# Four small moves around batch 0 of an adaLN block: row operations to GpSimd, exponentials ahead of q's seeds, far products ahead of a root, and ones in a TensorE wait

## The chip, the cores and the metric

The kernel runs as one program on one core of a Trainium2 chip. The metric is the device time of one execution in microseconds; the time before is the median of three runs. The four compute engines are TensorE (PE, with its weight loads as PEld), VectorE (DVE), ScalarE (ACT) and GpSimd (POOL). SyncE (SP) issues every DMA. Each engine takes its instructions in the order in which the program gives them, and waits only on semaphores.

## What is computed

Eight batches of 512 tokens with 256 features go through a modulated attention layer and a modulated, block-quantised linear layer:

```
mod = (silu(c) @ wmod).reshape(8, 6, 1, -1)
sa, ca, ga, sb, cb, gb = mod[:, 0] ... mod[:, 5]
ga = (2 * (ga >= 0) - 1) * maximum(abs(ga), 0.25)      # gb likewise
h = layernorm(x) * (1 + ca) + sa
x = x + ga * attention(h)      # 16 heads; only keys i and i - 2**k count, all others have score 0
h = layernorm(x) * (1 + cb) + sb
x = x + gb * (mx_quantize(h) @ mx_quantize(weight).T + bias)
```

Since each query sees only ten keys (offsets 0, 1, 2, 4 ... 256) beside a constant share of masked ones, the scores are ten elementwise products of q with a shifted k, summed over the 16 features of a head.

## The kernel before, in words

There is one loop over the batches, written out by hand for each engine, with the batches staggered: while the softmax of batch b is worked on, k, q and v of batch b + 1 and the transposes of batch b + 2 are made, and batch b - 1 is projected. What follows is the part around batch 0, where all edits lie.

**DVE.** It forms the products of batch 0 (`first_qk_products`, L1747), then `setup_rows` (L1711 to L1722): for all eight batches at once it takes the modulation rows out of PSUM and forms the clipped gates `rows8` and the gated biases `gated8`. These are operations on 8 partitions and 256 or 512 elements. Then comes `softmax_max(0)`: a maximum (L1833, tile `mx`) and, in two halves, the scores less that maximum (L1837). The maximum waits for the scores by token (`s_T`) and for both halves of `hT` of batch 1 (`s_hT` at 4). `softmax_weights(0)` (from L1850) waits for the exponentials, and `pv_product` (L1894) and `qk_product` (L1758) alternate after it.

**ACT.** After the scores and the two halves of `hT` of batch 1 (L1306), it seeds the banks of q with the bias (`seed_q(1)`, L1325), centres h of batch 1 (L1316, L1319), and only then enters the loop with `exps(0)` (em L1466, rest L1468, two halves L1471 and L1473). Then come `evacuate_k(1, ...)` (kT, L1332) and the statistics of batch 2: sums (L1231), squares (L1240), variance (L1244). The norm of batch 2 (x_norm, L1217) waits for POOL's root.

**POOL.** It splits the gated biases into three bf16 parts (`split_gated_biases`, L619 to L627), takes the root of batch 2 (`rstd_before(2)`: L662 with the operation pow, then L664), forms batch 0's two far products (`far_product`, L689: offsets 128 and 256), and adds up the products that DVE makes (`add`, L681). In batch b >= 1 the far products wait until TensorE has transposed the sums of batch b - 1 (`s_attp`).

**PE.** In batch 0 it makes k and q of batch 1 (L847, L858), v of batch 1 (L876), then waits for `x_norm` of batch 2 and transposes it (L834), turns one weight (L803), makes k of batch 2 (L847), and sums the products into scores of batch 1 (L980, L974, L994). `keep_busy` (L773) issues matmuls of ones whose result nobody reads.

**SP.** The DMA of the rows, `mod_rows<-x` (L510), stands behind the seven shifted loads of v.

The order on each engine is code order. The only things that couple them are the semaphores named here.

Of the kernel before, what the change touches and what calls it, by code (L numbers as in the profile page):

```python
# [5 lines left out]
ALU = mybir.AluOpType  # L6
# [20 lines left out]
def adaln_block(nc, x, wq, bq, wk, bk, wv, bv, wo, bo, wf, bf, cond, wmod, out):  # L27
    B, L, D = x.shape
# [41 lines left out]
    with ExitStack() as ctx:  # L70
# [24 lines left out]
        QUAD = 32  # L95
# [109 lines left out]
        s_wqk = sem("q_k_weights_transposed")  # L205
        s_xtile = sem("first_x_norm_tiles_by_scalar")
        s_xtiled = sem("first_x_norm_tiles_by_vector")
        s_split = sem("gated_biases_split")
        s_xin = sem("x_in_loaded")
        s_cols = sem("cols_loaded")  # L210
# [81 lines left out]
        CONST_EARLY = 7  # L292
        CONST_SUM = CONST_EARLY + 4 * NC
        CONST_ALL = CONST_SUM + NO + 1
        SETUP_SILU, SETUP_COLS, SETUP_WF, SETUP_MOD, SETUP_ROWS = 3, 5, 11, 12, 16
        PE_COND, PE_MOD, PE_WK, PE_COLS, PE_WQ, PE_WV, PE_ROWS, PE_WO, PE_WF = range(1, 10)
        NGATED = 5
        NLN1, NRS1, NLN2, NLN2D, NRS2 = 3, 2, 2, 3, 2
# [101 lines left out]
        def _(sp):  # L400
# [105 lines left out]
            for n in SHIFTED[1:]:  # L506
                shift_v(0, n)
            load_cols(2)
            sp.wait_ge(s_cset, SETUP_ROWS)
            sp.dma_start(rows_dram.ap(), rows8[:, :, :]).then_inc(s_spill, 16)  # L510
            sp.wait_ge(s_spill, 32)
            load_row_ga(0)
# [71 lines left out]
        def _(pool):  # L584
# [25 lines left out]
            for n in range(1, NO):  # L610
# [2 lines left out]
            nc.gpsimd.tensor_copy(fold[:, :].rearrange("p (y x h) -> p y x h", x=4, h=HC),  # L613
                                  ident[:, :].rearrange("p (x y h) -> p y x h", x=4, h=HC)).then_inc(s_const, 1)

            def split_gated_biases():

                pool.wait_ge(s_cset, SETUP_ROWS)
                nc.gpsimd.tensor_copy(split8[:, 0], gated8[:, :, :]).then_inc(s_split, 1)  # L619
                pool.wait_ge(s_split, 1)  # L620
                nc.gpsimd.tensor_tensor(rest8[:, :, :], gated8[:, :, :], split8[:, 0], ALU.subtract).then_inc(s_split, 1)
                pool.wait_ge(s_split, 2)
                nc.gpsimd.tensor_copy(split8[:, 1], rest8[:, :, :]).then_inc(s_split, 1)
                pool.wait_ge(s_split, 3)
                nc.gpsimd.tensor_tensor(rest8[:, :, :], rest8[:, :, :], split8[:, 1], ALU.subtract).then_inc(s_split, 1)
                pool.wait_ge(s_split, 4)
                nc.gpsimd.tensor_copy(split8[:, 2], rest8[:, :, :]).then_inc(s_split, 1)  # L627
# [82 lines left out]
            nc.gpsimd.memset(bias_att[:, :], 0.0).then_inc(s_bzero, 1)  # L710
            nc.gpsimd.memset(bias_ffn[:, :, :], 0.0).then_inc(s_bzero, 1)
            rstd_before(1)
            split_gated_biases()
            for b in range(LAST - 1):
                if has(b - 2):
                    rstd_after(b - 2)
                if has(b - 3):
                    dequantise_early(b - 3)
                if b == 0:
                    rstd_before(2)  # L720
                if b < EARLY:
                    far_product(b, 8)
                    far_product(b, 9)
                add(b, 1)
                if has(b - 2):
                    modulate(pool, nc.gpsimd, b - 2)
                if has(b - 3):
                    gate_ffn(b - 3)
                add(b, 2)
                add(b, 3)  # L730
                add(b, 4)
                add(b, 5)
                if has(b + 3):
                    rstd_before(b + 3)
                else:
                    rstd_after(b - 1)
                add(b, 6)
                if not has(b + 3):
                    dequantise_early(b - 2)
                add(b, 7)  # L740
                gate_projection(b)
# [23 lines left out]
        def _(pe):  # L765
# [371 lines left out]
            for b in range(LAST - 1):  # L1137
                ahead, post = has(b + 2), has(b - 3)
                q_rows(b + 1, 0)
                q_rows(b + 1, 1)  # L1140
                v_rows(b + 1, 1)
                if has(b - 1):
                    attention_transposes(b - 1)
                v_rows(b + 1, 0)
                if ahead:
                    h_transposes(b + 2, 1)
                    h_transposes(b + 2, 0)
                if b == 0:
                    weight_transposes(3)
                if has(b - 1):  # L1150
                    project(b - 1)
                if ahead:
                    k_rows(b + 2, 1)
                    k_rows(b + 2, 0)
                if post:
                    xd_transposes(b - 3)
                if b == 1:
                    weight_transposes(4)
                head_sums(b + 1, 0)
                if post:  # L1160
                    ffn(b - 3, 0)
                    ffn(b - 3, 1)
                head_sums(b + 1, 1)
                head_sums(b + 1, 2)
                scores_by_token(b + 1)
                if b in (0, 3):
                    v_means(means_of(b))
# [38 lines left out]
        def _(act):  # L1206
# [293 lines left out]
            copy_scores(0)  # L1500
            h_modulated(1, 1)
            h_modulated(1, 0)
            seed_q(1)
            centre_h(1)

            for b in range(LAST - 1):
                ahead, norm1 = has(b + 2), has(b + 3)
                exps(b)
                if b in (1, 4):
                    means_of_v(means_of(b - 1))  # L1510
                if b == 0:
                    evacuate_k(1, 1)
                    evacuate_k(1, 0)
                    sums_before(2)
                    squares_before(2)
                elif ahead:
                    norm_before(b + 2)
                if has(b - 2):
                    squares_after(b - 2)
                if has(b - 3):  # L1520
                    quantised(b - 3)
                evacuate_v(b + 1, 1)
                if b == 0:
                    norm_before(2)
                    evacuate_v(b + 1, 0)
                else:
                    evacuate_attention(b - 1)
                if has(b - 2):
                    norm_after(b - 2)
                if ahead:  # L1530
                    h_modulated(b + 2, 1)
                    h_modulated(b + 2, 0)
                if b == 0:
                    evacuate_weight(3)
                if norm1 and b > 0:
                    sums_before(b + 3)
                if has(b - 1):
                    take_x1(b - 1)
                if ahead:
                    evacuate_k(b + 2, 1)  # L1540
                    evacuate_k(b + 2, 0)
                if has(b - 3):
                    evacuate_xd(b - 3)
                    seed_ffn(b - 3)
                if ahead:
                    centre_h(b + 2)
                if b == 0:
                    sums_before(3)
                if norm1:
                    squares_before(b + 3)  # L1550
                if b == 1:
                    evacuate_weight(4)
                if not norm1:
                    squares_after(b - 1)
                if has(b - 3):
                    take_result(b - 3, 0)
                    take_result(b - 3, 1)

                copy_scores(b + 1)
                if ahead:  # L1560
                    seed_q(b + 2)
# [55 lines left out]
        def _(dve):  # L1617
# [87 lines left out]
            def setup_rows():  # L1705

                link, k = chain(s_cset, 0, 0)
                k[0] = SETUP_WF
                dve.wait_ge(s_pset, PE_ROWS)
                for i, m in enumerate((0, 3)):  # L1710
                    nc.vector.tensor_copy(gates[:, i, :], ps67[QUAD * m:QUAD * m + B, 0, 0:D])  # L1711
                nc.vector.tensor_copy(rows8[:, SB, :], ps67[QUAD:QUAD + B, 0, 0:D])
                link(nc.vector.tensor_scalar(rows8[:, CB, :], ps67[2 * QUAD:2 * QUAD + B, 0, 0:D], 1.0, None, ALU.add))
                assert k[0] == SETUP_MOD
                nc.vector.tensor_scalar(sgn[:, :, :], gates[:, :, :], 0.0, 2.0, ALU.is_ge, ALU.mult)
                link(nc.vector.tensor_scalar(mag[:, :, :], gates[:, :, :], -1.0, None, ALU.mult))
                link(nc.vector.scalar_tensor_tensor(out=mag[:, :, :], in0=gates[:, :, :], scalar=0.25,
                                                    in1=mag[:, :, :], op0=ALU.max, op1=ALU.max))
                link(nc.vector.scalar_tensor_tensor(out=rows8[:, GA:GB + 1, :], in0=sgn[:, :, :], scalar=-1.0,
                                                    in1=mag[:, :, :], op0=ALU.add, op1=ALU.mult))  # L1720
                dve.wait_ge(s_brow, 32)
                link(nc.vector.tensor_tensor(gated8[:, :, :], rows8[:, GA:GB + 1, :], brow[:, :, :], ALU.mult))  # L1722
                assert k[0] == SETUP_ROWS

            def setup_ffn_weight():
                link, k = chain(s_cset, 0, 0)
# [276 lines left out]
```

## Time and profile before

| | |
|---|---|
| median of three runs | 280.76 us (280.75 to 281.2) |
| the profiled execution's own time | 280.1 us |
| its span | 278.3 us |
| PE, DVE, ACT, POOL busy | 91%, 90%, 76%, 75% of the span |
| mean granted TensorE clock | 0.994 |

The profiled execution is 0.66 us shorter than the median, and 1.8 us of it lie outside the span. Busy shares are averages over the span; where a wait decides, the chain of work that ended last and the timelines of single engines say so.

### The profile page before, as it was taken

The page shows a single profiled execution, that of the slowest core. Times are in us where ns is not written, and L with a number is a line of the kernel's source. Part 1 is how long each engine was busy: PE and PEld are TensorE (multiplying, and loading weights), DVE is VectorE, ACT ScalarE, POOL GpSimd, SP SyncE. Part 2 cuts the span into 40 slices and gives each one's busy share as a digit, 9 for nine tenths or more (in the row PEclk, how much of TensorE's full clock was granted, in tenths as well). Part 3 has the DMA queues.
Part 4 walks back from the last instruction along what each step waited for, and adds up shares of the span by engine and source line. Part 5 has one row for each costly group of instructions (what it writes and reads, how often), then busy time and mean ns, then how long its engine had stood idle before and what let it go on. Part 6 is the DMA issues. An engine that isn't in the chain of part 4 may idle for free.

```text
span 278.3 us, 4396 instructions
## 1 busy us (share of the span) xinstructions
PE 253.6 (91%) x1356; PEld 162.7 (58%) x1356; DVE 249.4 (90%) x318; ACT 210.8 (76%) x564; POOL 209.4 (75%) x159
## 2 busy tenths in 40 slices
PE   6999996999999998799999999999999578997885
PEld 1754565258636843485568654766468445895664
DVE  3699899989998999999889998999984999999970
ACT  2377896785888896989889997998776736666753
POOL 6201339996998999999999899999999899945100
PEclk9999997999999999999999999999999999999999
DMA  7752996696695489327944796069803875730006
GB/s 226 191 194 78 297 312 179 205 351 196 212 320 182 141 273 319 127 98 252 341 143 132 221 361 197 19 204 364 247 1 116 255 212 180 227 133 15 0 5 224
DMA packets 54386, 53.90 MB, mean 194 GB/s; under 512 B 4094, under 2 KB 52812, under 8 KB 54364
## 3 DMA queue, kind: packets, MB, share of 16 engines
q1 hardware_dynamic: 54364, 53.63, 60.4%
q8 instruction: 11, 0.18, 0.3%
q14 instruction: 11, 0.09, 0.1%
HBM read 44.89 MB, written 8.72 MB: 193 GB/s over the span
## 4 chain that ended last, share of the span: by engine, by line
DVE 32%; PE 30%; ACT 14%; POOL 13%; issue 8%; DMA 1%; DVEq 0%; POOLq 0%; ACTq 0%
POOL pv_buf L681 7%; DVE prod L1758 6%; DVE pv_buf L1894 5%; PE ps L847 5%; PE ps L1111 5%; DVE prod L1894 4%; PE ps L1032 4%; DVE prod L1747 4%; PE ps L980 3%; ACT x_norm L1217 3%; ACT dump L1240 2%; PE ps L876 2%; POOL h L394 2%; POOL x_norm L389 2%; PE ps L834 2%
## 5 line engine op out<-in xcount | busy, mean ns | idle before, releaser
L681 POOL TENSOR_TENSOR pv_buf<-pv_buf 128x1024 f32<-128x1024 f32 x48 | 113.8, 2370 | 5.0 <-DVE pv_buf L1894 0.8
L1758 DVE TENSOR_TENSOR prod<-ps,kT 128x1024 f32<-128x1024 f32 (+4 forms) x70 | 75.0, 1107 | 0.0
L1894 DVE TENSOR_TENSOR pv_buf<-v_shift,ps 128x1024 f32<-128x1024 f32 x49 | 59.0, 1209 | 1.0 <-POOL pv_buf L681 1.0
L876 PE MATMUL ps<-wT,h_cen 128*128 128x256 f32 x128 | 29.9, 379 | 0.0
L847 PE MATMUL ps<-hT,wT 128*128 128x512 f32 x64 | 29.6, 603 | 0.0
L858 PE MATMUL ps<-hT,wT 128*128 128x512 f32 x64 | 29.4, 599 | 0.0
L876 PEld LDWEIGHTS ps<-wT,h_cen 128*128 128x128 f32 x128 | 23.9, 190 | 6.4 <-issue 3.8
L980 PE MATMUL ps<-prod,sel_sum 128*32 128x512 f32 x208 | 25.0, 598 | 2.0 <-DVE prod L1758 1.5
L1032 PE MATMUL ps<-wo_g,w_raw 128*128 128x256 f32 x112 | 26.4, 379 | 0.0
L662 POOL TENSOR_TENSOR rstd<-var,minus_half 128x4 f32<-128x4 f32 x8 | 8.1, 1017 | 20.5 <-ACT var L1244 19.0
L1032 PEld LDWEIGHTS ps<-wo_g,w_raw 128*128 128x128 f32 x112 | 21.2, 190 | 3.5
L858 PEld LDWEIGHTS ps<-hT,wT 128*128 128x128 f32 x64 | 11.7, 190 | 13.0 <-issue 12.4
L847 PEld LDWEIGHTS ps<-hT,wT 128*128 128x128 f32 x64 | 12.3, 198 | 11.9 <-issue 10.7
L1111 PE MATMUL ps<-wf_g,w_raw 128*128 128x256 f32 x80 | 18.7, 379 | 0.0
L670 POOL TENSOR_TENSOR rstd<-var,minus_half 128x4 f32<-128x4 f32 (+1 forms) x9 | 9.0, 998 | 11.5 <-ACT var L1285 8.8
L1332 ACT ACTIVATE kT<-ps,bias_cols 128x512 f32<-128x512 f32 x16 | 10.9, 687 | 8.7 <-PE ps L847 8.6
L1111 PEld LDWEIGHTS ps<-wf_g,w_raw 128*128 128x128 f32 x80 | 15.2, 190 | 2.3
L389 POOL TENSOR_TENSOR x_norm<-x_norm,rows_mod 128x1024 f32<-128x1024 f32 x6 | 14.2, 2365 | 1.9 <-ACT x_norm L1217 1.9
L1217 ACT ACTIVATE x_norm<-x_in,shift,rstd 128x256 f32<-128x256 f32 x28 | 14.5, 589 | 1.5 <-POOL shift L664 1.3
L1217 ACT ACTIVATE x_norm<-x,shift,rstd 128x256 f32<-128x256 f32 x28 | 14.5, 589 | 1.4 <-POOL shift L672 1.4
L394 POOL TENSOR_TENSOR h<-x_norm,rows_mod 128x1024 f32<-128x1024 f32 x6 | 14.2, 2362 | 0.5
L1306 ACT ACTIVATE hT<-ps,cols 128x512 f32<-128x512 f32 x16 | 12.2, 769 | 2.7 <-PE ps L821 2.0
(220 smaller groups left out, 570.7 us busy)
## 6 DMA issues: line engine op xcount, KB each, us to landing
v_shift<-v_rows SPq DMA_DIRECT2D x56, 512.0 KB, 5.5
x_in<-in_L_attn_x SPq DMA_DIRECT2D x8, 512.0 KB, 4.0
v_rows<-v_base SPq DMA_DIRECT2D x8, 512.0 KB, 3.0
x_res<-in_L_attn_x SPq DMA_DIRECT2D x8, 512.0 KB, 6.1
out_x<-outb SPq DMA_DIRECT2D x5, 512.0 KB, 4.7
rows_mod<-mod_rows SPq DMA_DIRECT2D x7, 256.0 KB, 6.1
x<-in_L_wmod SPq DMA_DIRECT2D x1, 1024.0 KB, 8.1
row_ga<-mod_rows SPq DMA_DIRECT2D x8, 128.0 KB, 3.0
```

Source lines behind the costliest of these rows:

```text
L389: ops.tensor_tensor(normed[:, t, :], normed[:, t, :], rows[:, 0:1, :].broadcast_to([P, n, D]), ALU.mult).then_inc(scaled, 1)
L394: ops.tensor_tensor(dst[:, t, :], normed[:, t, :], rows[:, 1:2, :].broadcast_to([P, n, D]), ALU.add).then_inc(done, 1)
L681: nc.gpsimd.tensor_tensor(dst, dst, ring(b, n)[:, t:NT, :], ALU.add).then_inc(s_add, 1)
L847: mm = nc.tensor.matmul(ps23[:, j, :], wT[:, 1, k, P * j:P * j + P], hT[:, k, :], start=(k == 1), stop=(k == 0))
L858: mm = nc.tensor.matmul(ps01[:, j, :], wT[:, 0, k, P * j:P * j + P], hT[:, k, :], start=False, stop=(k == NC - 1), skip_group_check=True)
L876: mm = nc.tensor.matmul(ps23[:, k2, col:col + D], h_cen[:, k, P * t:P * t + P], wT[:, 2, k, :], start=(t % 2 == 0 and k == 0), stop=(t % 2 ...
L980: mm = nc.tensor.matmul(ps23[32 * g:32 * g + 32, 1, :], sel_sum[:, which, c, :], prod[:, n, c, :], start=(c == 0 and which == 0), stop=(c ...
L1032: mm = nc.tensor.matmul(ps[:, k2, col:col + D], attnT[:, k, P * t:P * t + P], wo_by[b][:, k, :], start=False, stop=(t % 2 == 1 and k == NC ...
L1111: mm = nc.tensor.matmul(ps[:, half_, col:col + D], xdT_by[b][:, k, P * t:P * t + P], wf_by[b][:, k, :], start=False, stop=(t % 2 == 1 and ...
L1217: ins = nc.scalar.activation(dst[:, t, :], src[:, t, :], ACT.Identity, scale=rstd[:, t:t + 1], bias=shift[:, t:t + 1])
L1758: nc.vector.tensor_tensor(prod[:, n, :, o:L], ps01[:, :, o:L], kT[:, b % 2, :, 0:L - o], ALU.mult).then_inc(s_prod, 1)
L1894: nc.vector.tensor_tensor(dst[:, at, :].rearrange("p t (h e) -> p t h e", e=DH), v_n.rearrange("p t (h e) -> p t h e", e=DH), weights, ALU ...
```

## The change

Four edits, each in the setup or in the first two turns of the loop.

1. `setup_rows` on DVE ends two operations earlier. It now keeps twice the gate and a sign of plus or minus a half, so that the two remaining operations are plain products, and POOL does them: a new function `form_gates` with its own semaphore `s_gates`. SP's store of the rows waits for the first of them.
2. ACT does `seed_q(1)` and `centre_h(1)` after `exps(0)`, with the two halves of k between them.
3. POOL does `rstd_before(2)` after both far products and the first add of batch 0. In batch 1 the first add stands ahead of the far products.
4. PE issues six matmuls of ones after v of batch 1, ahead of the transposes of batch 2.

```diff
@@ sync
-            sp.wait_ge(s_cset, SETUP_ROWS)
+            sp.wait_ge(s_cset, SETUP_MOD)
+            sp.wait_ge(s_gates, 1)
@@ gpsimd
+            def form_gates():
+                pool.wait_ge(s_cset, SETUP_GATES)
+                nc.gpsimd.tensor_tensor(rows8[:, GA:GB + 1, :], sgn[:, :, :], mag[:, :, :], ALU.mult).then_inc(s_gates, 1)
+                pool.wait_ge(s_gates, 1)
+                pool.wait_ge(s_brow, 32)
+                nc.gpsimd.tensor_tensor(gated8[:, :, :], rows8[:, GA:GB + 1, :], brow[:, :, :],
+                                        ALU.mult).then_inc(s_gates, 1)
...
+            form_gates()
             split_gated_biases()
             for b in range(LAST - 1):
...
-                if b == 0:
-                    rstd_before(2)
+                if b == 1:
+                    add(b, 1)
                 if b < EARLY:
                     far_product(b, 8)
                     far_product(b, 9)
-                add(b, 1)
+                if b != 1:
+                    add(b, 1)
+                if b == 0:
+                    rstd_before(2)
@@ tensor
                 v_rows(b + 1, 0)
+                if b == 0:
+                    pe.wait_ge(s_d, 1)
+                    keep_busy(ps67, 0, 6)
@@ scalar
-            seed_q(1)
-            centre_h(1)
...
                 if b == 0:
+                    seed_q(1)
                     evacuate_k(1, 1)
+                    centre_h(1)
                     evacuate_k(1, 0)
@@ vector
-                    nc.vector.tensor_copy(gates[:, i, :], ps67[QUAD * m:QUAD * m + B, 0, 0:D])
+                    nc.vector.tensor_scalar(gates[:, i, :], ps67[QUAD * m:QUAD * m + B, 0, 0:D], 2.0, None, ALU.mult)
...
-                nc.vector.tensor_scalar(sgn[:, :, :], gates[:, :, :], 0.0, 2.0, ALU.is_ge, ALU.mult)
+                nc.vector.tensor_scalar(sgn[:, :, :], gates[:, :, :], 0.0, 0.5, ALU.is_ge, ALU.subtract)
...
-                link(nc.vector.scalar_tensor_tensor(out=rows8[:, GA:GB + 1, :], in0=sgn[:, :, :], scalar=-1.0,
-                                                    in1=mag[:, :, :], op0=ALU.add, op1=ALU.mult))
-                dve.wait_ge(s_brow, 32)
-                link(nc.vector.tensor_tensor(gated8[:, :, :], rows8[:, GA:GB + 1, :], brow[:, :, :], ALU.mult))
```

On ACT, between the second half of `hT` and the first sum of batch 2, stood before (`ps<-bias_cols` are q's seeds, `em` to the second `ps<-score_buf` are the exponentials):

```order
18 L1306 ACTIVATE hT,h_sum<-ps,cols 128x512 x2
19 L1325 ACTIVATE ps<-bias_cols 128x512 x2
20 L1316 ACTIVATE h_off<-h_sum 128x2
21 L1319 ACTIVATE h_cen<-hT,h_off 128x512 x2
22 L1466 ACTIVATE em<-mx 128x64
23 L1468 ACTIVATE ps<-em 128x4x16
24 L1471 ACTIVATE ps<-score_buf 128x2x160
25 L1473 ACTIVATE ps<-score_buf 128x2x160
26 L1332 ACTIVATE kT<-ps,bias_cols 128x512 x2
27 L1231 ACTIVATE dump,sum<-x_in 128x256 x4
```

In the same place of the changed kernel stands:

```order
18 L1323 ACTIVATE hT,h_sum<-ps,cols 128x512 x2
19 L1483 ACTIVATE em<-mx 128x64
20 L1485 ACTIVATE ps<-em 128x4x16
21 L1488 ACTIVATE ps<-score_buf 128x2x160
22 L1490 ACTIVATE ps<-score_buf 128x2x160
23 L1342 ACTIVATE ps<-bias_cols 128x512 x2
24 L1349 ACTIVATE kT<-ps,bias_cols 128x512
25 L1333 ACTIVATE h_off<-h_sum 128x2
26 L1336 ACTIVATE h_cen<-hT,h_off 128x512 x2
27 L1349 ACTIVATE kT<-ps,bias_cols 128x512
```

The number of instructions ahead of the sums is the same; the exponentials, which wait for DVE's maximum, are now the first of them.

On POOL, from the splits of the gated biases to the second root of the loop, stood before (`rstd` and `shift` are a root):

```order
39 L619 CAST split<-h 8x512
40 L621 TENSOR_TENSOR h<-h,split 8x512
41 L623 CAST split<-h 8x512
42 L625 TENSOR_TENSOR h<-h,split 8x512
43 L627 CAST split<-h 8x512
44 L662 TENSOR_TENSOR rstd<-var,minus_half 128x4
45 L664 TENSOR_TENSOR shift<-negmean,rstd 128x4
46 L689 TENSOR_TENSOR far_buf<-v_base,score_buf 128x768
47 L689 TENSOR_TENSOR far_buf<-v_base,score_buf 128x512
48 L681 TENSOR_TENSOR pv_buf<-pv_buf 128x1024 x5
```

and now stands:

```order
39 L620 TENSOR_TENSOR x<-outb 8x512
40 L623 TENSOR_TENSOR h<-x,zq 8x512
41 L629 CAST split<-h 8x512
42 L631 TENSOR_TENSOR h<-h,split 8x512
43 L633 CAST split<-h 8x512
44 L635 TENSOR_TENSOR h<-h,split 8x512
45 L637 CAST split<-h 8x512
46 L699 TENSOR_TENSOR far_buf<-v_base,score_buf 128x768
47 L699 TENSOR_TENSOR far_buf<-v_base,score_buf 128x512
48 L691 TENSOR_TENSOR pv_buf<-pv_buf 128x1024
49 L672 TENSOR_TENSOR rstd<-var,minus_half 128x4
50 L674 TENSOR_TENSOR shift<-negmean,rstd 128x4
```

Two products are new ahead of the splits, and the root went from ahead of the far products to behind them and one add.

## Rows read from the trace of the kernel before

**Rows 1.** Page, granted TensorE clock in 40 slices of the span.
```profile
PEclk9999997999999999999999999999999999999999
```

**Rows 2.** Chain of work that ended last, 30 to 60 us: start, us, what.
```profile
30.88 0.95 ACT hT L1306 x3
...
40.88 1.01 POOL rstd L662
...
50.73 0.04 ACT kT L1332
...
56.96 0.59 ACT score_buf L1482
```

**Rows 3.** Timeline of ACT, 31 to 62 us: start, us, operation, [idle before <-releaser].
```profile
31.73 1.11 ACT L1325 ACTIVATE ps<-bias_cols 128x512 f32<-128x512 f32 x2
...
34.23 0.24 ACT L1466 ACTIVATE em<-mx 128x64 f32<-128x64 f32 x1
...
35.38 1.24 ACT L1332 ACTIVATE kT<-ps,bias_cols 128x512 f32<-128x512 f32 x2
36.52 0.41 ACT L1231 ACTIVATE dump<-x_in 128x256 bf16<-128x256 f32 x1
...
40.59 0.20 ACT L1244 ACTIVATE var<-sq 128x4 f32<-128x4 f32 x1
...
45.47 0.78 ACT L1306 ACTIVATE hT<-ps,cols 128x512 f32<-128x512 f32 x1 [0.73 <-PE ps L834]
...
60.99 0.40 ACT L1348 ACTIVATE v_mean<-ps,bias_cols 128x3 f32<-128x3 f32 x2
```

**Rows 4.** Timeline of DVE, 30 to 61 us.
```profile
30.69 0.68 DVE L1719 SCALAR_TENSOR_TENSOR x<-outb 8x512 f32<-8x512 f32 x1
...
32.12 0.89 DVE L1833 TENSOR_REDUCE mx<-ps 128x64 f32<-128x704 f32 x1
...
35.22 0.50 DVE L1850 TENSOR_TENSOR ps<-ps,em 128x320 f32<-128x320 f32 x1 [1.29 <-ACT ps L1471]
...
58.77 0.89 DVE L1833 TENSOR_REDUCE mx<-ps 128x64 f32<-128x704 f32 x1 [0.78 <-PE ps L1011]
...
60.79 0.50 DVE L1850 TENSOR_TENSOR ps<-ps,em 128x320 f32<-128x320 f32 x1 [0.21 <-ACT ps L1471]
```

**Rows 5.** Timeline of POOL, 32 to 64 us.
```profile
32.15 0.60 POOL L619 CAST split<-h 8x512 bf16<-8x512 f32 x1 [7.41 <-DVE h L1722]
...
35.93 0.60 POOL L627 CAST split<-h 8x512 bf16<-8x512 f32 x1
...
42.11 2.51 POOL L689 TENSOR_TENSOR far_buf<-v_base,score_buf 128x768 f32<-128x768 f32 x2
44.59 12.43 POOL L681 TENSOR_TENSOR pv_buf<-pv_buf 128x1024 f32<-128x1024 f32 x5
...
63.19 1.27 POOL L639 TENSOR_TENSOR wo_g<-wT,row_ga 128x512 f32<-128x512 f32 x1
```

**Rows 6.** Timeline of SP's queue, the store of the rows.
```profile
36.09 0.35 SPq L510 DMA_DIRECT2D mod_rows<-x  x1
```

**Rows 7.** Timeline of PE: transposes, the wait before batch 2, ones and a wait near the end.
```profile
29.51 1.09 PE L834 MATMUL ps<-ident,x_norm 128*128 128x128 f32 x8
...
44.32 1.97 PE L834 MATMUL ps<-ident,x_norm 128*128 128x128 f32 x8 [2.53 <-ACT x_norm L1217]
...
219.67 0.38 PE L1081 MATMUL ps<-bias_ffn,ones 128*128 128x512 bf16 x1 [2.00 <-ACT ps L1428]
...
258.36 0.82 PE L773 MATMUL ps<-ones 3*128 3x512 bf16 x3
```

**Rows 8.** Windows: stretch, us, busy time of PE, PEld, DVE, ACT, POOL, granted clock, DMA share, GB/s.
```profile
43.75:44.00 0.25, 0.00 (x0) 0.00 (x0) 0.25 (x1) 0.25 (x2) 0.25 (x1) 0.67 0.61 201
44.00:47.00 3.00, 2.68 (x13) 2.68 (x14) 3.00 (x4) 2.27 (x5) 2.94 (x2) 0.50 0.73 197
...
47.25:50.75 3.50, 3.50 (x12) 1.29 (x15) 3.50 (x4) 1.23 (x3) 3.36 (x2) 1.00 1.03 354
```

More of the change, by code:

```diff
@@ L207, in adaln_block @@
         s_xtiled = sem("first_x_norm_tiles_by_vector")
+        s_gates = sem("gates_formed")
         s_split = sem("gated_biases_split")
@@ L294, in adaln_block @@
         CONST_ALL = CONST_SUM + NO + 1
-        SETUP_SILU, SETUP_COLS, SETUP_WF, SETUP_MOD, SETUP_ROWS = 3, 5, 11, 12, 16
+        SETUP_SILU, SETUP_COLS, SETUP_WF, SETUP_MOD, SETUP_GATES = 3, 5, 11, 12, 14
         PE_COND, PE_MOD, PE_WK, PE_COLS, PE_WQ, PE_WV, PE_ROWS, PE_WO, PE_WF = range(1, 10)
@@ L614, in _ @@
                                   ident[:, :].rearrange("p (x y h) -> p y x h", x=4, h=HC)).then_inc(s_const, 1)
+            def form_gates():
[5 more added lines that the diff above has]
+                                        ALU.mult).then_inc(s_gates, 1)
             def split_gated_biases():
-                pool.wait_ge(s_cset, SETUP_ROWS)
+                pool.wait_ge(s_gates, 2)
                 nc.gpsimd.tensor_copy(split8[:, 0], gated8[:, :, :]).then_inc(s_split, 1)
@@ L1714, in setup_rows @@
                 assert k[0] == SETUP_MOD
-                nc.vector.tensor_scalar(sgn[:, :, :], gates[:, :, :], 0.0, 2.0, ALU.is_ge, ALU.mult)
+                nc.vector.tensor_scalar(sgn[:, :, :], gates[:, :, :], 0.0, 0.5, ALU.is_ge, ALU.subtract)
                 link(nc.vector.tensor_scalar(mag[:, :, :], gates[:, :, :], -1.0, None, ALU.mult))
-                link(nc.vector.scalar_tensor_tensor(out=mag[:, :, :], in0=gates[:, :, :], scalar=0.25,
+                link(nc.vector.scalar_tensor_tensor(out=mag[:, :, :], in0=gates[:, :, :], scalar=0.5,
                                                     in1=mag[:, :, :], op0=ALU.max, op1=ALU.max))
-                link(nc.vector.scalar_tensor_tensor(out=rows8[:, GA:GB + 1, :], in0=sgn[:, :, :], scalar=-1.0,
-                                                    in1=mag[:, :, :], op0=ALU.add, op1=ALU.mult))
-                dve.wait_ge(s_brow, 32)
-                link(nc.vector.tensor_tensor(gated8[:, :, :], rows8[:, GA:GB + 1, :], brow[:, :, :], ALU.mult))
-                assert k[0] == SETUP_ROWS
+                assert k[0] == SETUP_GATES
             def setup_ffn_weight():
```

## The prediction

> **What bounds the kernel now.** I read the chain of work that ended last first, from the end of batch 0's scores to the scores of batch 1, since all edits lie there. It runs through ACT, not DVE: from the second half of hT, which ends at 31.83, ACT works without a gap through q's seeds, centring, exponentials, k and batch 2's statistics up to the variance at 40.59 [rows 2, 3]. POOL's root follows at 40.88, ACT's norm, and PE's transposes of batch 2 at 44.32 [rows 2, 7]. From there the chain goes through k of batch 2 (kT at 50.73) and the next statistics on ACT to the copy of batch 1's scores at 56.96 [rows 2]. DVE is not on it: ahead of the maximum of batch 1, at 58.77, it has been idle for 0.78 us, waiting for PE's transposes of those scores [rows 4]. A microsecond saved on DVE before that point only makes this wait longer. A microsecond lost on ACT ahead of the root goes straight into the end.
>
> Then the clock. It dips once in the whole span, in the seventh slice [rows 1]. PE had been idle for 2.53 us before 44.32 [rows 7]. In the stretch 43.75 to 44.00 the mean is 0.67, so it fell to its lower level, 1.2 GHz, at about 43.8, two microseconds into the wait; it stays at 0.50 to about 47.25 and is back at 1.00, 2.4 GHz, after it [rows 8].
>
> **The change, part by part.**
>
> *Two operations off DVE.* They took 32.12 - 30.69 = 1.43 us [rows 4]. But the maximum also needs hT, done at 31.83 [rows 2]; add some 0.05 for the signal, and it starts at 31.9 in place of 32.12. The cut is worth 0.2 us of its 1.43.
>
> *Exponentials first on ACT.* ACT is free at 31.83, where q's seeds start at 31.73 today by overlap [rows 3]. Now em has to wait for the maximum: 31.9 + 0.89, so 32.8. ACT stands still for 1.1 us where it had no gap. In batch 1, where the exponentials also meet DVE at work, the ACT operation behind them starts 60.99 - 58.77 = 2.22 us after the maximum [rows 3, 4]; here that is 34.1. Before, the exponentials took ACT 35.38 - 34.23 = 1.15 us, seeds and centring 34.23 - 31.73 = 2.50, k 36.52 - 35.38 = 1.14 [rows 3]. The sums of batch 2 therefore start at 34.1 + 2.50 + 1.14 = 37.75 against 36.52, and the variance is there at 42.0 against 40.79: a loss of 1.25 us on the chain. For DVE the move is a gain: L1850 came 2.02 us after the maximum in batch 1 [rows 4], so at 33.9 here against 35.22, 1.3 us earlier. Seeds now end near 34.7 and 35.2; the matmuls of q that add to them are behind k on PE and start at about 34.7, so nothing waits there by more than 0.1 us (PE is reckoned as busy up to 44.32 - 2.53 = 41.79 either way [rows 7]).
>
> *Row operations on POOL.* The gates are ready for POOL at 30.7 [rows 4]. A product of 512 elements took POOL 1.27 us [rows 5], on 128 partitions; the split, on 8 partitions, ran five operations from 32.15 to 36.53 [rows 5], 0.6 to 1.2 each. I take 1.2 to 1.3 for each product, 2.5 for both. The split then runs 33.2 to 37.6. SP's store of the rows went out at 36.09, behind the loads of v [rows 6], and its input is now there at 32; the store of the split biases is behind it in the same queue. Nothing on SP moves.
>
> *Root behind far products and an add.* POOL does the far products at 37.7 (42.11 to 44.59, so 2.48 us [rows 5]), and the add (12.43 / 5 = 2.49 us [rows 5]). That is the root at 42.65. The variance would have let it start at 42.1; the order costs 0.5 more. In all the root moves from 40.88 to 42.65, by **1.77 us**, and so do norm and transposes: PE starts on batch 2 at 46.1. The other five adds of batch 0 get ahead of their old places by 3 us, but the root of batch 3 stands in front of the last two and waits for ACT, as it nearly does today. The exchange in batch 1 starts an add while the far products would wait for PE; POOL then meets the root of batch 4, which waits for ACT again. Both are worth nothing.
>
> *Ones.* Three took 0.82 us at the full clock, so 0.22 each after the first [rows 7]; six end at 43.1, inside the wait. They cost nothing on the chain. They leave PE idle from 43.1 to 46.1, 3.0 us.
>
> *What the clock is worth.* From the transposes to kT of batch 2 takes 50.73 - 44.32 = 6.41 us [rows 2, 7]. PE worked for 2.7 to 2.9 us of it at 0.50 [rows 8]; at 1.00 this is 1.35 to 1.45 less. The eight transposes show it: 1.97 against 1.09 [rows 7]. Part of it is hidden, since k's matmuls also wait for hT from ACT (0.78 for a half [rows 3]), which does not get faster. I take 1.25.
>
> A rule of the Trainium skill bears on this ("TensorE: Matmul & The Clock Gate", Part 4: PE-mode transpose): transposes don't count as TensorE activity as matmuls do, so they would not bring the clock back. The trace does not agree: most of the work between 44.32 and the return at 47.25 was transposes. By the rule a low stretch would last longer here; the fourth case below is that one.
>
> **The sum.** With the clock held: +1.77 - 1.25 = +0.5 us. With a second fall in the longer wait, as now: +1.77 if the low stretch lies as it does today, and +0.5 + 1.7 = +2.2 if it comes fully under work (3.4 us at half speed costs 1.7; today 0.5 of it is spent idle). Behind 57 us everything follows ACT and PE as today, so this goes to the end unchanged.
>
> **The cases.**
>
> 1. *The clock falls again*, chance 0.53, +1.8 to +2.2. For it: an idle stretch of 2.53 us lost the clock after two [rows 7, 8], and this one is 3.0 us, after ones that use 3 of 128 rows of the array. Against it: a wait of 2.00 us near the end did not lose it [rows 7, 1], and where in a wait it falls is known from one fall only. The profiled execution, 280.1, would become 282.1; the median stands 0.66 above it, which gives **282.7**. Its own range is 282.0 to 283.4.
> 2. *The ones hold the clock*, chance 0.30: +0.5, so 281.3, from 280.7 to 281.8, just about the 0.2% (0.56 us) that a measurement of this kernel can tell from no change.
> 3. *Faster*, chance 0.10. The mechanism is DVE's 1.3 us reaching the end, with the clock held. It needs the copy of batch 1's scores before 56.4, hence transposes of batch 2 at full clock before 45.0 and the root before 41.6: the sums would have to start by 37.3, and POOL to be free 1.1 us earlier than reckoned. This happens if the maximum does not have to wait and the 8-partition products take next to nothing. At most 1.3 us: 279.5.
> 4. *A long low stretch*, chance 0.07: the clock falls in the wait and stays low through all of k of batch 2. The 3.5 us of matmul after 47.25 [rows 8] would take up to 7, on top of case 1: up to +5, 285.5.
>
> **Range and chances.** Slower by over 0.2%: all of cases 1 and 4 and a little under half of case 2, 0.73. Within: the rest of case 2 and a part of 3, 0.17. Faster: 0.10. The range goes from 280.6, below case 2's value, to 283.8, above that of case 1; it leaves out most of cases 3 and 4.
>
> **What the changed profile would show.** The maximum of batch 0 near 31.9, with ACT idle for 1 us before em; L1850 near 33.9. The first sum of batch 2 near 37.75, the root near 42.65 with POOL busy up to it, transposes of batch 2 near 46.1, PE idle for 3 us before them. DVE's wait ahead of batch 1's maximum grows from 0.78 to over 2.5. The windows of 43 to 51 us decide between cases 1, 2 and 4: a low granted clock or none. The forecast is wrong if ACT does not stand still ahead of em, if the root comes before 42, or if no low clock appears after the ones.

## The result and the profile after

The changed kernel takes 286.16 us (285.32 to 286.47, four executions) against 280.75 for the kernel before: a ratio of 1.0191, 95% interval 1.0165 to 1.0217. The prediction was 282.7, with a range to 283.8: the right side, but the loss is 5.4 us and not 2. Executions of one kernel here differ mostly by how often the TensorE clock fell in them, so the mean granted clock stands beside times below where it matters; in all four executions of the changed kernel it was 0.976.

Page of the changed kernel, span and granted clock in 40 slices:

```profile
span 284.5 us, 4409 instructions
PEclk9999997978999999999999999999999999999799
```

[rows 1] had one dip; here are three places: the seventh slice, the ninth and tenth, and one near the end.

DVE of the changed kernel, its timeline:

```profile
32.12 0.89 DVE L1846 TENSOR_REDUCE mx<-ps 128x64 f32<-128x704 f32 x1 [1.31 <-ACT hT L1323]
...
34.14 0.50 DVE L1863 TENSOR_TENSOR ps<-ps,em 128x320 f32<-128x320 f32 x1 [0.21 <-ACT ps L1488]
...
61.63 0.89 DVE L1846 TENSOR_REDUCE mx<-ps 128x64 f32<-128x704 f32 x1 [4.71 <-PE ps L1025]
...
89.56 0.89 DVE L1846 TENSOR_REDUCE mx<-ps 128x64 f32<-128x704 f32 x1 [3.14 <-PE ps L1025]
```

The maximum of batch 0 starts at the same 32.12 [rows 4]: it waited 1.31 us for hT, so most of the 1.4 us cut from DVE turned into a wait. (hT itself ended 0.16 us later in this execution, 31.99 against 31.83, ahead of any of the edits; the run with the row operations alone, below, has the maximum 0.14 us earlier.) L1863 (L1850 before) is 1.1 us earlier. All of that, and 2.9 us more, is spent in the wait ahead of batch 1's maximum, 4.71 us against 0.78.

ACT and POOL, their timelines:

```profile
33.04 0.26 ACT L1483 ACTIVATE em<-mx 128x64 f32<-128x64 f32 x1 [1.06 <-DVE mx L1846]
...
42.05 0.20 ACT L1261 ACTIVATE var<-sq 128x4 f32<-128x4 f32 x1
...
59.08 0.58 ACT L1499 ACTIVATE score_buf<-ps 128x512 f32<-128x512 f32 x1
```

```profile
30.89 1.27 POOL L620 TENSOR_TENSOR x<-outb 8x512 f32<-8x512 f32 x1 [6.31 <-DVE outb L1734]
32.24 1.26 POOL L623 TENSOR_TENSOR h<-x,zq 8x512 f32<-8x512 f32 x1
...
40.40 2.37 POOL L691 TENSOR_TENSOR pv_buf<-pv_buf 128x1024 f32<-128x1024 f32 x1
42.73 1.01 POOL L672 TENSOR_TENSOR rstd<-var,minus_half 128x4 f32<-128x4 f32 x1
```

ACT stands still for 1.06 us ahead of em, the variance comes at 42.05 to 42.25, and the root at 42.73, right behind the add (40.88 in [rows 2]). The copy of batch 1's scores, L1499, is at 59.08 against 56.96 [rows 2].

PE's timeline of the changed kernel, two rows of the kernel before in the same place, and windows of the changed kernel with the columns of [rows 8]:

```profile
42.12 1.46 PE L787 MATMUL ps<-ones 3*128 3x512 bf16 x6
46.18 1.97 PE L848 MATMUL ps<-ident,x_norm 128*128 128x128 f32 x8 [2.60 <-ACT x_norm L1234]
...
54.48 1.92 PE L988 MATMUL ps<-prod,sel_sum 128*32 128x512 f32 x16
56.19 1.06 PE L1008 MATMUL ps<-prod,sel_sum 128*32 128x512 f32 x8
59.71 1.02 PE L1020 MATMUL ps<-ident,score_buf 128*128 128x128 f32 x4 [2.45 <-ACT score_buf L1499]
...
62.95 5.52 PE L872 MATMUL ps<-hT,wT 128*128 128x512 f32 x8
```

```profile
52.36 3.87 PE L974 MATMUL ps<-prod,sel_sum 128*32 128x512 f32 x16
...
57.59 0.66 PE L1006 MATMUL ps<-ident,score_buf 128*128 128x128 f32 x4 [0.50 <-ACT score_buf L1482]
```

```profile
46.50:49.50 3.00, 3.00 (x13) 2.64 (x12) 3.00 (x4) 2.27 (x6) 2.86 (x2) 0.50 0.96 302
50.00:57.25 7.25, 7.25 (x47) 2.25 (x45) 6.91 (x7) 5.00 (x15) 3.73 (x2) 1.00 0.57 195
57.25:59.50 2.25, 0.01 (x2) 0.00 (x0) 0.00 (x0) 2.22 (x10) 0.25 (x1) 1.00 1.12 344
60.00:66.50 6.50, 6.50 (x20) 4.44 (x19) 4.53 (x9) 4.77 (x13) 6.28 (x5) 0.50 0.86 273
265.00:268.00 3.00, 3.00 (x8) 2.31 (x7) 2.86 (x7) 2.48 (x7) 1.34 (x2) 0.50 0.00 0
```

The first low stretch, 46.2 to 49.6, lies wholly under work; in the kernel before it began inside the wait.

The new event is the second wait. PE begins batch 1's sums 2.1 us late (52.73 against 50.62), but they take it 4.5 us and not 6.5: in the kernel before it had to wait for DVE's products among them (3.87 us for L974, 1.92 for the same L988 now). So they end at 57.25, nearly as before (57.09), while ACT copies the scores 2.1 us later, at 59.08. PE idles for 2.45 us where it idled for 0.5, and then works from 60.0 to 66.5 at 1.2 GHz. Eight matmul instructions of q take 5.52 us where they took 3.7 in the kernel before.

How the 6.2 us of span come about, by landmarks of the two profiles: kT of batch 2 at 52.84 against 50.73 (+2.1), maximum of batch 1 +2.9, maximum of batch 2 at 89.56 against 84.15 (+5.4), unchanged up to batch 6, and the rest at the end, where a third low stretch lies under matmuls.

### The profile page after: what moved, and what is told of

The parts are those of the page before. It is cut to its first block, busy times and chain, and to the rows that moved or that the text cites. A ratio compares the mean times of both kernels' runs of the same rounds, so it can differ in the third digit from the quotient of the medians.

```text
span 284.5 us, 4409 instructions
## 1 busy us (share of the span) xinstructions
PE 257.3 (90%) x1362; PEld 166.0 (58%) x1362; DVE 248.0 (87%) x316; ACT 211.3 (74%) x564; POOL 211.9 (74%) x161
## 4 chain that ended last, share of the span: by engine, by line
PE 34%; POOL 22%; ACT 15%; DVE 15%; issue 11%; DMA 2%; SPq 0%; POOLq 0%; ACTq 0%; DVEq 0%
POOL pv_buf L691 11%; PE ps L1125 6%; PE ps L861 6%; DVE prod L1907 4%; PE ps L1046 4%; ACT x_norm L1234 3%; PE ps L994 3%; DVE prod L1771 3%; PE ps L872 2%; POOL x_norm L390 2%; DVE pv_buf L1907 2%; ACT dump L1298 2%; ACT dump L1257 2%; DMA pv_buf<-in_L_wmod 2%; PE ps L890 2%
## 5 line engine op out<-in xcount | busy, mean ns | idle before, releaser
L872 PE MATMUL ps<-hT,wT 128*128 128x512 f32 x64 | 31.3, 632 | 0.0
L861 PE MATMUL ps<-hT,wT 128*128 128x512 f32 x64 | 29.4, 600 | 0.1
L1125 PE MATMUL ps<-wf_g,w_raw 128*128 128x256 f32 x80 | 20.0, 397 | 0.0
L861 PEld LDWEIGHTS ps<-hT,wT 128*128 128x128 f32 x64 | 12.1, 195 | 11.9 <-issue 10.7
L1125 PEld LDWEIGHTS ps<-wf_g,w_raw 128*128 128x128 f32 x80 | 16.2, 203 | 2.9 <-issue 0.3
L1846 DVE TENSOR_REDUCE mx<-ps 128x64 f32<-128x704 f32 x8 | 7.1, 891 | 11.1 <-PE ps L1025 9.6
L1358 ACT ACTIVATE v_base<-ps 128x512 f32<-128x512 f32 x16 | 9.3, 588 | 7.8 <-PE ps L890 6.7
```

Of the source, the lines that this page charges most:

```text
L861: mm = nc.tensor.matmul(ps23[:, j, :], wT[:, 1, k, P * j:P * j + P], hT[:, k, :], start=(k == 1), stop=(k == 0))
L872: mm = nc.tensor.matmul(ps01[:, j, :], wT[:, 0, k, P * j:P * j + P], hT[:, k, :], start=False, stop=(k == NC - 1), skip_group_check=True)
L1125: mm = nc.tensor.matmul(ps[:, half_, col:col + D], xdT_by[b][:, k, P * t:P * t + P], wf_by[b][:, k, :], start=False, stop=(t % 2 == 1 and ...
```

## The experiments

**The change, ones out.** 

```diff
-                if b == 0:
-                    pe.wait_ge(s_d, 1)
-                    keep_busy(ps67, 0, 6)
```

> The changed kernel without its six matmuls of ones. Theory T (two waits of TensorE each lose the clock: the one ahead of batch 2's transposes, and a new one of 2.45 us ahead of batch 1's scores): the ones end 2.6 us before work comes, so they hold nothing; 285.5 to 287, both low stretches still there. Rival R (the ones do hold something, or they disturb): more than 1 us slower or faster than 286.2.

284.53 us, ratio 1.0155 (1.0117 to 1.0193). Both low stretches are there, at 44.6 and at 58.2 for 6.8 us; the wait ahead of batch 1's scores is 2.46 us. The time is 1 us under the expectation and 1.6 us under the changed kernel's, which by the number alone is rival R. What the profile has less than the changed kernel is the third stretch near the end (0.9 us) and 0.9 us ahead of batch 0's maximum, at 31.24, where the clock rose earlier in this execution (10.4 us against 12.1). The one of its four executions with a mean clock of 0.976 took 286.09. So six ones held neither of the two stretches. Three of the executions here have a mean clock of 0.982 and none of the changed kernel's has; no run shows whether the ones have to do with that.

**The change with ScalarE's old order.**

```diff
             h_modulated(1, 0)
+            seed_q(1)
+            centre_h(1)
...
                 if b == 0:
-                    seed_q(1)
                     evacuate_k(1, 1)
-                    centre_h(1)
```

> The changed kernel with ScalarE's old order (q's seeds and centring ahead of the exponentials). Theory T: the far weights come 1 us later, so GpSimd's root, behind two far products and an add, is no earlier than now (43.3 us); transposes of batch 2 near 46.8; both low stretches stay; 285 to 287. Rival R (ScalarE's standing still ahead of em is by itself what the time hangs on): the root comes near 41 and the time is 282 or less.

286.64 us, ratio 1.0221 (1.0192 to 1.0250): no gain. Transposes start at 46.45, and both falls are there; the first stretch is 6.8 us long here (45.4 to 52.2). With the root behind far products and add, the old order of ACT by itself brings nothing back.

This run also bears on what opens the second wait. Its DVE and PE:

```profile
51.75 3.62 DVE L1771 TENSOR_TENSOR prod<-ps,kT 128x960 f32<-128x960 f32 x4
...
61.13 0.66 PE L1020 MATMUL ps<-ident,score_buf 128*128 128x128 f32 x4 [2.46 <-ACT score_buf L1499]
```

The execution is 0.54 us ahead of the kernel before at batch 0's maximum (31.58 against 32.12); against that, DVE's last products of batch 1 are no earlier than before (52.12 there). The wait is as long as in the changed kernel all the same. So a late k of batch 2 (here 4.1 us later than before, by the same measure) is enough for it; DVE does not have to be early. In the changed kernel k is 2.1 us late, and by the rows that is enough too: PE comes to the last sums, L1008, at 56.19, and DVE's products were done at 55.7 even in the kernel before. No run has that by itself.

**The change with the root first.**

```diff
+                if b == 0:
+                    rstd_before(2)
...
                     add(b, 1)
-                if b == 0:
-                    rstd_before(2)
```

> The changed kernel with the root of batch 2 ahead of the far products again. Theory T: the root starts as soon as the variance is there, 42.3 in place of 42.7; transposes at 45.7; the wait ahead of batch 1's scores shrinks from 2.45 to 2.0 us, which may or may not lose the clock: 285.5 if it does, 282.3 if it does not. Rival R (the root's place on GpSimd carries most of the loss): below 282.

Median 285.42 us; the recorded ratio, 1.0039 (0.9989 to 1.0088), is that of the three shortest executions alone. Transposes at 45.77, 0.4 earlier, as expected. The wait ahead of batch 1's scores did not shrink: 2.47 us, where 2.0 was expected, since PE's sums and ACT's copy both follow k of batch 2 (the copy 6.2 us behind the start of kT here, in the changed kernel and in the kernel before). Of ten executions two had a mean clock of 1.000 and took 280.60 and 280.74; one at 0.982 took 284.16; seven at 0.976 to 0.980 took 284.88 to 286.32. It is the same kernel with the same orders, so what lies between 280.7 and 285.5 goes with the clock. Theory T's better case, 282.3, had only the second stretch gone; in these two both are.

**Ones in both waits, 3 rows.**

```diff
-                    keep_busy(ps67, 0, 6)
+                    keep_busy(ps67, 0, 18)
...
+                if b == 0:
+                    pe.wait_ge(s_d, 1)
+                    keep_busy(ps67, 1, 10)
                 scores_by_token(b + 1)
```

> The changed kernel with 18 matmuls of ones in the first wait and 10 more ahead of batch 1's scores, so that TensorE is hardly idle in either. Theory T: with ones that count as activity neither low stretch appears, 281 to 282.3, and the transposes of batch 2 take 1.09 us in place of 1.97. Rival R (matmuls of ones on 3 rows of the array do not hold the clock): both stretches stay, 286 or more.

285.87 us, ratio 1.0195 (1.0149 to 1.0241). PE's timeline and windows of this run:

```profile
41.80 4.05 PE L787 MATMUL ps<-ones 3*128 3x512 bf16 x18
45.82 1.14 PE L848 MATMUL ps<-ident,x_norm 128*128 128x128 f32 x8
```

```profile
42.00:45.75 3.75, 3.75 (x18) 1.49 (x16) 3.75 (x4) 2.51 (x6) 3.67 (x4) 1.00 0.53 146
47.00:50.00 3.00, 3.00 (x7) 1.55 (x6) 3.00 (x4) 1.63 (x5) 2.86 (x2) 0.50 0.94 309
61.00:67.00 6.00, 6.00 (x11) 3.07 (x12) 5.62 (x10) 3.62 (x10) 5.17 (x3) 0.50 0.81 256
```

PE is busy without a gap and the clock falls all the same, at 46.9 and 60.5. That is rival R.

**Ones in both waits, 128 rows.** As above, with a second function `keep_busy_full` for these two places, whose operands (the rest of the call is cut here) are on all rows:

```diff
-ones3[0:NSPLIT, 0:P], ones3[0:NSPLIT, :].unsqueeze(1).broadcast_to([NSPLIT, NT, P])
+ones3[:, 0:P], ones3[:, :].unsqueeze(1).broadcast_to([P, NT, P])
```

> The changed kernel with ones in both waits (18 and 10 matmuls), now on all 128 rows of the array in place of 3. Theory T (two low stretches of the clock make up most of the loss, and ones on 3 rows do not count as work): no low clock between 40 and 70 us, 281 to 282, that is the delay of GpSimd's root less the gain of the held clock, +0.5 us. Rival R (the loss is in the order of ScalarE's and GpSimd's work, the clock only goes with it): 285 or more even with a full clock.

280.70 us (12 executions, mean clock 0.993 to 0.998), ratio 1.0007 (0.9993 to 1.0020).

```profile
41.85 4.05 PE L792 MATMUL ps<-ones 128*128 128x512 bf16 x18
45.95 1.14 PE L853 MATMUL ps<-ident,x_norm 128*128 128x128 f32 x8
```

```profile
47.00:50.00 3.00, 2.95 (x11) 1.52 (x10) 3.00 (x4) 2.17 (x6) 2.86 (x2) 1.00 0.96 298
61.00:67.00 6.00, 6.00 (x32) 4.31 (x31) 5.65 (x9) 4.08 (x10) 3.90 (x3) 1.00 1.05 340
```

The ones take the same time as on 3 rows and the clock stays. With it 5.2 us come back: the loss is the clock. The new orders with the clock held here, against the old ones with their one low stretch, have the maximum of batch 3 at 110.94 against 110.35, 0.6 us, in these two executions; by the medians it is 0.2 us, and the interval takes in no difference.

**128-row ones in the second wait only.**

```diff
+                if b == 0:
+                    pe.wait_ge(s_d, 1)
+                    keep_busy_full(ps67, 1, 10)
                 scores_by_token(b + 1)
```

> The changed kernel with 10 matmuls of ones on all 128 rows in the second wait only (ahead of batch 1's scores); the first wait keeps its six ones on 3 rows. Theory T: the low stretch of 59.8 to 66.7 us and its price of 3.3 us go, the first one stays with its price of about 1.3: 281.5 to 283. Rival R (both stretches cost alike, or the second costs little): 284 or more.

282.82 us, ratio 1.0073 (1.0052 to 1.0094). The first stretch is there (46.5 to 49.9), the second is not; batch 2's maximum is at 86.06 against 89.56. Eight of twelve executions took 282.7 to 283.1 at a mean clock near 0.988, four at 0.994 took 280.8 to 281.6.

**128-row ones in the first wait only.**

```diff
-                    keep_busy(ps67, 0, 6)
+                    keep_busy_full(ps67, 0, 18)
```

> The changed kernel with 18 matmuls of ones on all 128 rows in the first wait only. Theory T: the first low stretch goes, but the second wait, which comes from VectorE being early and ScalarE late, still loses the clock: 283 to 285. Rival R (the second fall was a consequence of the first): about 280.7, as with ones in both waits.

283.33 us, ratio 1.0092 (1.0061 to 1.0124). PE's row ahead of batch 1's scores:

```profile
58.19 0.66 PE L1025 MATMUL ps<-ident,score_buf 128*128 128x128 f32 x4 [2.34 <-ACT score_buf L1504]
```

The wait is there without the first fall, and loses the clock by itself (60.5 to 63.9) in this execution; one of the six, with a mean clock of 1.000, took 280.86. It is not a consequence of the first. Its length is another matter: 3.4 us here, and 6.8 us in all five profiled executions in which it came behind a first one. Batch 2's maximum is at 86.44, 1.7 us behind that of the run with both waits filled (84.74), so this stretch alone costs 1.7 us, and behind a first one 3.3.

Here DVE's head start does matter: k of batch 2 is only 0.6 us late (kT at 51.33), and DVE's last products start at 50.88, 1.2 us earlier than before. At their old time PE would have waited for them as it did in the kernel before. That is read from the rows; no run has it by itself.

**The kernel before, 11 ones on 128 rows in its wait.**

```diff
                 v_rows(b + 1, 0)
+                if b == 0:
+                    pe.wait_ge(s_d, 1)
+                    keep_busy_full(ps67, 0, 11)
```

> The kernel before with 11 matmuls of ones on all 128 rows in its 2.53 us wait, nothing else. Theory T: the low stretch of 43.8 to 47.2 goes, transposes of batch 2 take 1.09 us, and the time falls by 1.25 us, to 279.2. Rival R (the wait that follows on ScalarE takes it back): within 0.3 us of before.

280.15 us, ratio 0.9978 (0.9962 to 0.9993): 0.2%, not 0.45%. Transposes take 1.14 us, but batch 1's maximum is at 58.66 against 58.77. PE's waits between 40 and 60 us say why:

```profile
PE ps L979 <- DVE prod L1766: 1.1, 1, 1.1
```

PE, now early, stands and waits for DVE's products; rival R named ScalarE for this. ACT's second copy of the scores, behind those sums, starts at 57.32 where it started at 57.44 in the kernel before, with DVE 0.16 us later in this execution. So DVE was next in line there by 0.3 us, and a held clock can give back no more than about that.

**The kernel before, its own ones on 128 rows.** The diff is the operands above, in `keep_busy`; the first two ones (L768) stay on 3 rows, and nothing is in the middle.

> The kernel before with its own ones (2 + 3 + 4 at the start without the first two, 3 near the end) on all 128 rows, and none in the middle. Theory T: the clock rises near 9 us in place of 13, worth 1.2 us: 279 to 279.5, that is most of the gain of the run with all ones on 128 rows. Rival R: the gain there came from the middle: within 0.3 us of before.

279.11 us, ratio 0.9950 (0.9932 to 0.9968). Batch 0's maximum is at 30.67 against 32.12. PE in its first microseconds:

```profile
4.71 1.89 PE L773 MATMUL ps<-ones 128*128 128x512 bf16 x4
7.49 0.64 PE L786 MATMUL ps<-pv_buf,siluT 128*32 128x128 f32 x16 [0.90 <-DMA pv_buf<-in_L_wmod]
```

The 16 instructions of L786 take 0.64 us where the kernel before, with 3-row ones ahead of them, took 1.08; the clock rises at 6.6 us, not 13.1. In kernels with 3-row ones the rise came between 10.4 and 13.1 us, so it moves from execution to execution as well.

**All ones on 128 rows, and 11 in the wait.** Both of the last two edits together.

> The same as the run with 11 ones on all rows in the kernel before, and also the ones at the start and near the end on all 128 rows. Theory T: the clock also rises earlier at the start (it is at its lower level up to 13 us although TensorE issues ones from 2 us on), worth 1 to 2 us: 277.5 to 278.5. Rival R: no more than the 11 ones alone.

278.86 us, ratio 0.9941 (0.9919 to 0.9963), 0.4 us above what was expected: nearly all of the gain is the start.

**Row operations alone.** The kernel before with `form_gates` and the exchange of batch 1, and no ones in the wait.

> Of the change only the row operations on GpSimd and the exchange of batch 1's first add with its far products; ScalarE's order, the root ahead of the far products, and no new ones, as before. Theory T: the maximum starts at most 0.25 us earlier, nothing else moves: -0.2 us, so 280.2 to 280.7. Rival R (the two products on GpSimd are part of the loss): more than 0.5 us slower.

279.88 us, ratio 0.9978 (0.9966 to 0.9990). Batch 0's maximum is 0.14 us earlier than before. PE's row ahead of batch 2 in this run:

```profile
44.35 1.14 PE L848 MATMUL ps<-ident,x_norm 128*128 128x128 f32 x8 [2.54 <-ACT x_norm L1231]
```

The wait is as long as in the kernel before (2.53), it is not filled, and the clock did not fall in this execution: its mean is 1.000 and the transposes take 1.14 us. A full clock in a single profile is therefore no proof that ones held it; in the pair of runs on 3 and on 128 rows it is all the executions that differ (0.976 to 0.982 against 0.993 to 0.998).

**The best version.** Row operations, exchange, all ones on 128 rows (again without the first two), 11 in the wait; ScalarE's order and the root's place are those of the kernel before.

> Row operations on GpSimd and the exchange in batch 1, ones on all 128 rows at the start, near the end and 11 in the wait ahead of batch 2's transposes. Theory T: the two gains add: 278.1 to 278.5. Rival R: no better than the ones alone, 278.9.

278.00 us, ratio 0.9928 (0.9903 to 0.9952): 0.7% less than the kernel before and, by the two ratios, 2.6% less than the changed one. The interval overlaps that of the run with all ones on 128 rows and the old row operations (0.9919 to 0.9963), so what the row operations add to the ones isn't shown.

## Why the prediction was right in its direction and wrong in its size

**Up to 53 us it held.** The 0.2 us that the cut on DVE was worth (0.14 in the run with it alone), ACT's standstill (1.1 forecast, 1.06), the products on POOL (1.2 to 1.3, 1.27), the root (42.65, 42.73), the transposes (46.1, 46.18), the clock lost again (at 46.2, just as the wait ended), and kT of batch 2 (+1.8 to +2.2, +2.1) are as worked out. The idle stretch behind the ones is 2.60 us and not 3.0: they started 0.3 us later than reckoned and took 1.46 us for 1.3. The 1.25 us for the first low stretch fit the changed kernel: batch 1's maximum is at 60.68 with it and 59.36 without it, each with the second wait filled.

**The step that failed** is the last sentence of the sum: "Behind 57 us everything follows ACT and PE as today, so this goes to the end unchanged." The prediction had DVE 1.3 us early and ACT about 2 us late at the same place, and asked only what this does to DVE. PE stands between the two. In the kernel before it waited for DVE's products while it summed, and had only 0.5 us left to wait for ACT's copy. Once k of batch 2 is 2 us late the products lie ready, PE sums without a stop, and its whole slack towards ACT, 2.45 us, falls in one wait, in which it loses the clock a second time. That costs 3.3 us: batch 2's maximum at 86.06 with this wait filled against 89.56, less 0.24 by which that execution was ahead at batch 0. Half of it is the stretch's length, 6.8 us in place of the 3.4 that a stretch took so far; why it is double behind a first stretch stays open. The third stretch, near the end, costs another 0.9 us: from batch 7's maximum to the end the changed kernel needs 44.9 us, the one with both waits filled 44.0. It is also in the profiles of the runs with only one of the two waits filled on 128 rows. Why the clock falls there in some executions and not in others wasn't tried.

**The sum as it is:** orders 0.6, first stretch 1.3, second 3.3, third 0.9: 6.1 of the 6.2 us of span. These are differences between single profiled executions. The ratios say the same with less detail: 0.2 us for the orders with both waits filled, 1.8 more with the first stretch (the profile of that run has the third one too), 3.3 more with the second.

**Case 2 was sized right** for the orders (+0.5, measured 0.6 in the profiles and 0.2 in the medians), and named for the wrong reason: ones on 3 rows don't hold the clock. **Case 4** gave 285.5, near the measured time, by another mechanism; that is chance. (Its own terms, 3.5 us on top of 1.8 to 2.2, make 5.3 to 5.7 and so about 286.) A stretch through all of k of batch 2, as it describes, came in the run with ScalarE's old order, and not in the changed kernel.

**The 1.25 us** that a held clock gives back hold in the changed kernel, where DVE is early. They are not there to be had in the kernel before, where DVE is next in line by 0.3 us: holding the clock there gained 0.2%. Unfilled, the kernel before itself had a mean clock of 1.000 in four of the 17 executions measured beside the last runs; they took 280.0 to 280.5 us, no less than those at 0.994 (279.7 to 280.2).

The Trainium skill ("TensorE: Matmul & The Clock Gate", Part 1) says that a hardware block sets the clock by how busy TensorE has been. The runs agree, if busy means work on the array: 18 matmuls back to back on 3 rows did not count, on 128 rows they did.

## What to carry to other kernels

When work moves against the engine that feeds it or empties it, look at the engine between them. Short waits that were spread over its work can fall together into one long wait, and that can cost more than the shift itself, on TensorE by the clock (3.3 us here for a shift of 2.1). Fill such waits with matmuls on the whole array, and read the granted clock behind the filling, not TensorE's busy share. And before a wait is moved ahead on a full engine, ask when what it waits for is there: cutting 1.4 us of DVE brought the maximum no further than hT let it.

## What the runs showed of the hardware that was not expected

- Ones with a contraction over 3 partitions keep TensorE's records busy but neither hold the clock (3.75 us without a gap, then 0.50) nor raise it at the start (the rise came at 10.4 to 13.1 us, against 6.6 and 9.3 in two runs with 128 rows).
- A low stretch inside the run was either 3.4 or 6.8 us long. The second was 6.8 us in the changed kernel and in the four other profiles that had one ahead of it, and 3.4 us in the one that had none.
- The length of a wait does not say whether the clock falls. One of 2.53 us lost it in the kernel before and one of 2.54 us in the run with the row operations alone did not. The wait of 2.00 us near 219 us kept it in the kernel before, and the same wait lost it in the run with both waits filled (220.6 to 224.0, at no cost to batch 7's maximum).
- The same kernel, the one with the root first, took 280.6 us with a mean clock of 1.000 and 286.3 us with 0.976.
